# Cross-attentions: half of the next pair's first turning round on either side of a weighting's last block of keys

## The chip, the cores and the metric

The kernel runs on one core of a Trainium2 chip. Its time is the device time of one launch in microseconds (us): 1676.99 us as the median of 3 runs (1670.87 to 1678.79). Engines are called as in the profile: PE (TensorE, matmuls), PEld (TensorE's weight loads), PEldq (its queue of instructions), DVE (VectorE), ACT (ScalarE), POOL (GpSimd), SP (the queue of DMAs).

## The reference

Four decoder layers run one after the other on a batch of 8 sequences of 56 tokens, 256 wide, each layer with a self-attention, an attention or another mixing over the outside context `ctx_512`, and a feed-forward block, each with a residual and a layer norm. Layers 0, 2 and 3 have a cross-attention of the same form (16 heads, latent keys of width 64, 1500 keys):

```
scores = einsum('bhsr,bhlr->bhsl', q_r, k_r)
attn   = softmax(scores, axis=-1)
ctx_c  = einsum('bhsl,bld->bhsd', attn, kv_rope)
out    = einsum('bhsd,hkd->bshk', ctx_c, w_kc_kv).reshape(b, s, H*K) @ Wo.T
```

All three run through the same function of the kernel, `cross_attention`, and this is the only function that the change touches.

## The kernel before, in words

**Pairs.** The 8 sequences go in 4 couples (`j`, two sequences `e` = 0 and 1, one on partitions 0 to 63 and one on 64 to 127 of the operands). 16 heads times 56 tokens are 896 rows of scores for each sequence, cut into 7 pieces of 128 rows. One piece for both sequences of a couple is a pair in the sense of this document: `NU` = 28 pairs `i` in each cross-attention, 84 in the kernel. In every seventh (`u` = 3, `SPLIT`) the 128 rows belong to two halves of the heads, so that the weighting has four parts of 64 columns where it has two of 128 otherwise. Below these are the split pairs.

**Steps of a pair.** (1) `score` (L1019): six matmuls of 64 rows and 500 columns fill PSUM banks 0 to 2 (`e` = 0) and 3 to 5 (`e` = 1). The profile shows each as two records. (2) `rowmax` on DVE (L1299, L1301, L1304): row maxima, for `e` = 0 bank by bank, for `e` = 1 in one. (3) `exp` on ACT (L1220): one for each `e`, with the row sum read out after it. (4) `normalise` on DVE (L1308, L1312). (5) `turn` on PE (L1106): the weights are transposed in blocks of 125 keys, 24 blocks of two transposes each (one from partitions 0 to 63, one from 64 to 127), in three rounds `k` of 8 blocks. Round 0 writes banks 0 and 1, the banks of the scores of `e` = 0. (6) The copies of the turned blocks to SBUF: round 0 by DVE (L1318), rounds 1 and 2 by ACT (L1227). (7) `weigh` on PE (L1119): for 12 blocks of keys, the context (125 rows, 64 columns) is the stationary operand and the turned weights stream past. Two parts of a block write the two halves of the columns of bank 6, and each is again two records. The last one raises `pv_mm`. (8) `keep` on DVE (L1325) copies bank 6 away, and POOL (L892) sets it in place.

**Order on PE.** It is written out by hand: in step `i` of the loop PE issues `score(i)`, then `weigh(i - 2)`, then the three rounds of `turn(i - 1)`. The 26 steps with `i` from 2 to 27 have all three, so there are 78 in the kernel. Round 0 waits (L1092, L1094) for both divisions of its own pair and for the first exp of the pair scored last, since that exp still reads banks 0 to 2. Round 2 waits for `kept` (L1096), since it writes bank 6, and for the second exp of the pair scored last (L1101). On DVE the order in step `i` is: row maxima of `i`, division `e` = 0, `keep(i - 2)`, the two copies of turned blocks of `i - 1`, division `e` = 1. On ACT: both exps of `i`, then four copies of `i - 1`.

```
        for i in range(1, NU):
            for k in range(3):
                score(i, k)
            ...
            if i >= 2:
                weigh(i - 2)
            for k in turn_order(i - 1):
                turn(i - 1, k)
```

After the loop the last pairs, the projections (L1134) and the norms follow, and the change leaves them alone.

Of the kernel before, what the change touches and what calls it, by code (L numbers as in the profile page):

```python
# [25 lines left out]
L, LC, LT = 1500, 64, 12  # L26
# [138 lines left out]
def keep_busy(c, bank, n, rhs=None, cols=512):  # L165


    rhs = c.ctx_feat[:, 0, :] if rhs is None else rhs
    for _ in range(n):
        c.nc.tensor.matmul(c.ps[:, bank, 0:cols], c.ident[:], rhs[:, 0:cols], start=True, stop=True, skip_group_check=True)  # L170
# [578 lines left out]
def cross_attention(c, name, o, rope, now, prefetch):  # L749
# [19 lines left out]
    else:  # L769
# [33 lines left out]
    maxed, turned_lo, turned_hi, d_in, a_in, pv_mm, kept, ct_in, ct_last = (  # L803
        s.sem(x) for x in ("maxed", "turned_lo", "turned_hi", "d_in", "a_in", "pv_mm", "kept", "ct_in", "ct_last"))
# [8 lines left out]
    def turn_bank(i, k, r):  # L813

        if i == 0:
            return ((0, 1), (2, 5), (6, 7))[k][r]
        if i == NU - 1:
            return ((2, 3), (4, 7), (6, 5))[k][r]
        return ((0, 1), (2, 7), (6, 5))[k][r]
# [14 lines left out]
    def turn_order(i):  # L834

        return (2, 0, 1) if i == 0 else (0, 1, 2)
# [15 lines left out]
    def parts(u):  # L852

        if u == SPLIT:
            return [(0, 0, 0, 64), (1, 1, 0, 64), (0, 1, 64, 128), (1, 0, 64, 128)]
        return [(0, 0, 0, 128), (1, 1, 0, 128)] if u < SPLIT else [(1, 0, 0, 128), (0, 1, 0, 128)]
# [39 lines left out]
    def _(pe):  # L896
# [108 lines left out]
        def score(i, k):  # L1005

            if i == 0 and k < 2:
                pe.wait_ge(cm_act.handle, cm_act.at(2 - k))
            if i > 0 and k == 0:
                for e in range(2):  # L1010
                    pe.wait_ge(exped[e].handle, exped[e].at(i))
            if i > 1 and k < 2:
                pe.wait_ge(d_in.handle, d_in.at(2 * (i - 2) + 1 + k))
            if i > 1 and k == 2:
                pe.wait_ge(a_in.handle, a_in.at(4 * (i - 2) + 3))
            j, u = i // UNITS, i % UNITS
            q = q2[:, j, :, :].rearrange("p h t -> p (h t)")[:, u * 128:(u + 1) * 128]
            for e in range(2):
                m = nc.tensor.matmul(sc[e][:, k, :], q[e * 64:(e + 1) * 64],  # L1019
                                     c.ctx_feat[e * 64:(e + 1) * 64, j, k * 4 * LP:(k + 1) * 4 * LP],  # L1020
                                     start=True, stop=True)
                if e == 0:
                    m.then_inc(*scored[0].next())
                elif k == score_order(i)[-1]:
                    m.then_inc(*scored[1].next())
# [59 lines left out]
        out_of_context(2)  # L1085
        out_of_context(3)

        def turn(i, k):

            if k == turn_order(i)[0]:  # L1090
                for e in range(2):
                    pe.wait_ge(normed[e].handle, normed[e].at(i + 1))  # L1092
            if k == 0 and i < NU - 1:
                pe.wait_ge(exped[0].handle, exped[0].at(i + 2))  # L1094
            if k == 2 and i > 0:
                pe.wait_ge(kept.handle, kept.at(i))  # L1096
            if i == 0 and k == 2:
                pe.wait_ge(lat_in.handle, lat_in.at(4 * NH // 2))
                pe.wait_ge(cm_act.handle, cm_act.at(3))
            if k == (1 if i == 0 else 2) and i < NU - 1:  # L1100
                pe.wait_ge(exped[1].handle, exped[1].at(i + 2))  # L1101
            for n in range(8):
                e, l = divmod(8 * k + n, LT)
                for r in range(2):
                    rows = slice(r * 64, (r + 1) * 64)
                    m = nc.tensor.transpose(c.ps[0:LP, turn_bank(i, k, r), n * 64:(n + 1) * 64],  # L1106
                                            probs[i % 2][e][rows, l * LP:(l + 1) * LP], c.ident[rows, rows])
                    if n == 7:
                        m.then_inc(*(turned_hi if r else turned_lo).next())

        def weigh(i):

            j, u = i // UNITS, i % UNITS
            pe.wait_ge(a_in.handle, a_in.at(4 * (i + 1)))
            pe.wait_ge(d_in.handle, d_in.at(2 * (i + 1)))
            y = c.ps[:, 6, :]
            for l in range(LT):
                for r, e, lo, hi in parts(u):
                    m = nc.tensor.matmul(y[r * 64:(r + 1) * 64, lo:hi], c.ctx_pos[:, j, l, e, :],  # L1119
                                         pT[i % 2][:, lo // 64:hi // 64, LT * e + l, :], start=(l == 0 and lo == 0),  # L1120
                                         stop=(l == LT - 1), skip_group_check=True)
            m.then_inc(*pv_mm.next())

        def project(j):

# [13 lines left out]
# [3 lines that stand above are left out]
            if i == 1:  # L1142

                pe.wait_ge(cm_act.handle, cm_act.at(3))
                keep_busy(c, 6, 1)
                keep_busy(c, 6, 1, None, 256)
            if i >= 2:
                weigh(i - 2)
            for k in turn_order(i - 1):
                turn(i - 1, k)  # L1150
        pe.wait_ge(d_in.handle, d_in.at(2 * (NU - 1)))
        project(0)
        weigh(NU - 2)
        project(1)
        for k in range(3):
            turn(NU - 1, k)
        project(2)
        weigh(NU - 1)
        for j in range(3):
            norm_turn(c, s, pe, j)  # L1160
# [1804 lines left out]
```

## Time and profile before

| what | value |
|---|---|
| median of 3 runs | 1676.99 us (1670.87 to 1678.79) |
| the profiled execution, its own time | 1670.51 us |
| its span, first to last instruction | 1668.7 us |
| PE busy | 1624.9 us, 97% of the span |
| DVE busy | 1112.9 us, 67% |
| ACT busy | 748.2 us, 45% |
| POOL busy | 239.3 us, 14% |
| mean granted clock of TensorE | 0.993 of full speed |

The table is an average over stages. Weight loads (PEld) overlap the matmuls. The end of a matmul in the profile is modelled, and successive ones overlap, so a start less the start before it is the time that a matmul takes in a stream, and the duration given for one record is longer than that. The time outside the span is 1670.51 - 1668.7 = 1.8 us.

### The profile page before, as it was taken

Reading aid. Unit: us, or ns where it says so; the run is one execution under the profiler, and the core shown is the slowest. Engines: PE = TensorE matmul, PEld = TensorE weight load, DVE = VectorE, ACT = ScalarE, POOL = GpSimd, SP = SyncE. Lnnn points to the kernel's source line nnn. Section 1 sums busy time; section 2 is a strip of 40 time slices with the busy share of each in tenths; the row PEclk is TensorE's granted clock in tenths of the full one; section 3 lists DMA queues with packets and bytes.
Section 4 is the critical chain, followed back from the end, with each engine's and each line's share of the span. In section 5 each row is a group of like instructions: output and inputs, shape, how many; then the busy total and the mean of one; then the engine's idle time right before and its main releaser. Section 6 shows DMA issues by size and latency. Waiting matters only on the chain.

```text
span 1668.7 us, 35613 instructions
## 1 busy us (share of the span) xinstructions
PE 1624.9 (97%) x15226; PEld 1104.2 (66%) x15226; DVE 1112.9 (67%) x1964; ACT 748.2 (45%) x1288; POOL 239.3 (14%) x428
## 2 busy tenths in 40 slices
PE   8999999999999889999999999999999999999998
PEld 5575367777755656655367777764566767777765
DVE  2735899999566753266899999535445289999632
ACT  2213366666412641134366666312444366666411
POOL 0011200000010313011200000010455000000030
PEclk9999999999999999999999999999999999999999
DMA  9212020000040011051020000050300220000010
GB/s 279 73 26 82 1 77 2 2 2 2 2 187 1 2 59 40 1 118 63 1 96 2 2 2 2 2 241 1 64 1 1 114 89 2 2 2 2 2 45 11
DMA packets 35494, 71.10 MB, mean 43 GB/s; under 512 B 25331, under 2 KB 29747, under 8 KB 31405
## 3 DMA queue, kind: packets, MB, share of 16 engines
q1 hardware_dynamic: 35338, 68.83, 12.7%
q8 instruction: 121, 1.98, 0.5%
q14 instruction: 35, 0.29, 0.1%
HBM read 68.36 MB, written 0.46 MB: 41 GB/s over the span
## 4 chain that ended last, share of the span: by engine, by line
PE 90%; DVE 5%; ACT 2%; issue 1%; DMA 1%; POOL 1%; ACTq 0%; DVEq 0%; SPq 0%; POOLq 0%
PE ps L1106 14%; PE ps L1119 14%; PE ps L1019 13%; PE ps L351 10%; PE ps L1478 9%; PE ps L930 3%; PE ps L2549 3%; PE ps L1134 3%; PE ps L513 2%; PE ps L1918 2%; PE ps L940 1%; PE ps L2576 1%; PE ps L966 1%; PE ps L951 1%; PE ps L508 1%
## 5 line engine op out<-in xcount | busy, mean ns | idle before, releaser
L1220 ACT ACTIVATE arena<-ps,softmax_stats 128x1500 f32<-128x1500 f32 x168 | 254.0, 1512 | 192.8 <-DVE softmax_stats L1301 190.8
L1119 PEld LDWEIGHTS ps<-arena,ctx_pos 125*64 125x64 f32 x4608 | 222.3, 137 | 58.4 <-issue 55.4
L1106 PE MATMUL ps<-ident,arena 64*125 64x64 f32 x4032 | 239.2, 271 | 1.9 <-ACT arena L1220 1.6
L1119 PE MATMUL ps<-arena,ctx_pos 125*64 125x128 f32 (+1 forms) x4608 | 240.5, 262 | 0.0
L1106 PEld LDWEIGHTS ps<-ident,arena 64*125 64x125 f32 x4032 | 226.8, 185 | 17.0 <-issue 13.5
L1019 PE MATMUL ps<-ctx_feat,arena 64*128 64x500 f32 x1008 | 230.5, 590 | 0.0
L1227 ACT COPY arena<-ps 125x512 f32<-125x512 f32 x336 | 172.5, 599 | 77.8 <-PE ps L1106 77.8
L1299 DVE TENSOR_REDUCE softmax_stats<-ps 128x1 f32<-128x500 f32 x252 | 170.7, 678 | 48.9 <-PE ps L1019 48.5
L351 PE MATMUL ps<-arena 128*128 128x256 f32 x736 | 174.6, 383 | 2.9 <-ACT arena L2644 1.0
L1312 DVE TENSOR_SCALAR arena<-arena,softmax_stats 128x1500 f32<-128x1500 f32 x168 | 168.3, 1002 | 5.9
L1478 PE MATMUL ps<-x_feat,arena 128*128 128x448 f32 (+1 forms) x416 | 166.2, 544 | 1.2 <-DVE arena L1579 1.2
L351 PEld LDWEIGHTS ps<-arena 128*128 128x128 f32 x736 | 137.0, 190 | 40.2 <-issue 16.9
L892 POOL COPY arena<-arena 64x128 f32<-64x128 f32 (+1 forms) x186 | 51.3, 276 | 682.1 <-DVE arena L1325 675.9
L1304 DVE TENSOR_REDUCE softmax_stats<-ps 128x1 f32<-128x1500 f32 x84 | 143.6, 1709 | 0.0
L1019 PEld LDWEIGHTS ps<-ctx_feat,arena 64*128 64x128 f32 x1008 | 89.2, 187 | 80.0 <-issue 77.1
L1478 PEld LDWEIGHTS ps<-x_feat,arena 128*128 128x128 f32 (+1 forms) x416 | 78.7, 191 | 64.6 <-issue 60.6
L1318 DVE COPY arena<-ps 125x512 f32<-125x512 f32 x168 | 107.6, 682 | 12.8 <-PE ps L1106 12.5
L1545 ACT ACTIVATE arena<-ps 128x448 f32<-128x448 f32 (+1 forms) x52 | 28.3, 544 | 193.0 <-PE ps L1478 192.9
L1579 DVE TENSOR_TENSOR arena<-ps,arena 128x448 f32<-128x448 f32 x45 | 28.1, 624 | 129.5 <-ACT arena L1545 94.6
L930 PE MATMUL ps<-x_feat,arena 128*128 128x448 f32 x128 | 56.1, 563 | 0.2
L2549 PE MATMUL ps<-x_feat,arena 128*128 128x448 f32 x128 | 52.4, 552 | 1.2 <-issue 0.7
L2677 DVE TENSOR_TENSOR arena<-ps,arena 128x448 f32<-128x448 f32 x32 | 20.0, 625 | 46.0 <-ACT arena L2621 45.9
(319 smaller groups left out, 1923.4 us busy)
## 6 DMA issues: line engine op xcount, KB each, us to landing
ctx_pos<-in_ctx SPq DMA_DIRECT2D x1, 2688.0 KB
arena<-in_L1f_gate SPq DMA_DIRECT2D x1, 2304.0 KB, 12.0
arena<-in_L1f_up SPq DMA_DIRECT2D x1, 2304.0 KB, 17.0
arena<-in_L1f_down SPq DMA_DIRECT2D x1, 2304.0 KB, 7.8
arena<-in_L0a_Wq SPq DMA_DIRECT2D x1, 2048.0 KB, 10.5
arena<-in_L0a_Wc SPq DMA_DIRECT2D x1, 2048.0 KB, 19.4
arena<-in_L0x_Wq SPq DMA_DIRECT2D x1, 2048.0 KB, 10.1
arena<-in_L0x_Wo SPq DMA_DIRECT2D x1, 2048.0 KB, 8.4
```

The source lines that it names most:

```text
L351: m = c.nc.tensor.matmul(y_of(c, s, j), lhsT, rhs, start=False, stop=last, skip_group_check=True)
L930: m = nc.tensor.matmul(c.ps[:, 2 + h % 2, 0:NT], wq[:, k, h, :], c.x_feat[:, k, :, 0:T], start=(k == 0), stop=(k == KT - 1))
L1019: m = nc.tensor.matmul(sc[e][:, k, :], q[e * 64:(e + 1) * 64], c.ctx_feat[e * 64:(e + 1) * 64, j, k * 4 * LP:(k + 1) * 4 * LP], start=True ...
L1106: m = nc.tensor.transpose(c.ps[0:LP, turn_bank(i, k, r), n * 64:(n + 1) * 64], probs[i % 2][e][rows, l * LP:(l + 1) * LP], c.ident[rows, r ...
L1119: m = nc.tensor.matmul(y[r * 64:(r + 1) * 64, lo:hi], c.ctx_pos[:, j, l, e, :], pT[i % 2][:, lo // 64:hi // 64, LT * e + l, :], start=(l = ...
L1220: nc.scalar.activation(probs[i % 2][e].rearrange("p (k l) -> p k l", k=3), sc[e], ACT.Exp, bias=low[:, i % 4, e:e + 1], accum_out=total[:, ...
L1227: nc.scalar.copy(pT[i % 2][:, r, 8 * k:8 * k + 8, :], c.ps[0:LP, turn_bank(i, k, r), :].rearrange("p (s q) -> p s q", s=8)).then_inc(*a_in ...
L1299: nc.vector.tensor_reduce(peak[:, i % 4, k:k + 1], sc[0][:, k, :], AX.X, ALU.max).then_inc(*maxed.next())
L1304: nc.vector.tensor_reduce(low[:, i % 4, 1:2], sc[1], AX.XY, ALU.max, negate=True).then_inc(*lowered[1].next())
L1312: nc.vector.tensor_scalar(probs[i % 2][e], probs[i % 2][e], inv[:, i % 4, e:e + 1], None, ALU.mult).then_inc(*normed[e].next())
L1318: nc.vector.tensor_copy(pT[i % 2][:, r, 0:8, :], c.ps[0:LP, turn_bank(i, 0, r), :].rearrange("p (s q) -> p s q", s=8)).then_inc(*d_in.next())
L1478: m = nc.tensor.matmul(c.ps[0:m_, bank(n) + i, 0:NT], w[:, k, n * 128:n * 128 + m_], c.x_feat[:, k, :, 0:T], start=(k == 0), stop=(k == KT ...
```

## The change

Step `i` of the loop, from `i` = 2 on, calls `weigh_and_turn(i - 2)`. PE then issues: the weighting's blocks of keys 0 to 10; the waits of turning round 0; the first 4 blocks of that round (8 transposes); the weighting's last block of keys, 11; the other 4 blocks of the round; rounds 1 and 2 as before. Step 1 and all that comes after the loop keep their order. The instructions, operands, banks and semaphores are the same ones. The other engines' programs are unchanged.

```
-        def turn(i, k):
+        def turn_ready(i, k):
             ... (the waits of turn, as before)
-            for n in range(8):
+
+        def turn_blocks(i, k, ns):
+
+            for n in ns:
                 e, l = divmod(8 * k + n, LT)
                 ...
+        def weigh_keys(i, ls):
+
+            j, u = i // UNITS, i % UNITS
             y = c.ps[:, 6, :]
-            for l in range(LT):
+            for l in ls:
                 for r, e, lo, hi in parts(u):
                     m = nc.tensor.matmul(...)
-            m.then_inc(*pv_mm.next())
+            if LT - 1 in ls:
+                m.then_inc(*pv_mm.next())
...
+        def weigh_and_turn(i):
+
+            weigh_ready(i)
+            weigh_keys(i, range(LT - 1))
+            turn_ready(i + 1, 0)
+            turn_blocks(i + 1, 0, range(4))
+            weigh_keys(i, [LT - 1])
+            turn_blocks(i + 1, 0, range(4, 8))
+            for k in (1, 2):
+                turn(i + 1, k)
...
             if i >= 2:
-                weigh(i - 2)
-            for k in turn_order(i - 1):
-                turn(i - 1, k)
+                weigh_and_turn(i - 2)
+            else:
+                for k in turn_order(i - 1):
+                    turn(i - 1, k)
```

## Rows read from the trace of the kernel before

**Rows 1.** Busy time of each engine in the loop of the first cross-attention.

```profile
core 0: us, PE busy (x) PEld busy (x) DVE busy (x) ACT busy (x) POOL busy (x), PEclk, DMA share, GB/s
226.60:435.30 208.70, 208.70 (x2990) 163.30 (x2988) 191.76 (x310) 135.27 (x206) 16.52 (x60) 1.00 0.01 3
```

**Rows 2.** The page's chain of work that ended last, by engine.

```profile
PE 90%; DVE 5%; ACT 2%; issue 1%; DMA 1%; POOL 1%; ACTq 0%; DVEq 0%; SPq 0%; POOLq 0%
```

**Rows 3.** Timeline of PE, one pair's period: start us, us, engine, line.

```profile
389.22 2.84 PE L1119 MATMUL ps<-arena,ctx_pos 125*64 125x128 f32 x48
391.99 2.83 PE L1106 MATMUL ps<-ident,arena 64*125 64x64 f32 x48
394.66 2.73 PE L1019 MATMUL ps<-ctx_feat,arena 64*128 64x500 f32 x12
397.33 0.88 PE L1119 MATMUL ps<-arena,ctx_pos 125*64 125x128 f32 x12
```

**Rows 4.** L1119's and L1106's records, 389 to 398 us: ns minimum/median/maximum.

```profile
L1119 PE MATMUL ps<-arena,ctx_pos x60: 272/273/323, 389.2 to 397.9; 125*64 125x128 f32 x60
L1106 PE MATMUL ps<-ident,arena x48: 269/269/317, 392.0 to 394.6; 64*125 64x64 f32 x48
```

**Rows 5.** Timeline of PE, a split pair.

```profile
421.64 3.02 PE L1119 MATMUL ps<-arena,ctx_pos 125*64 125x64 f32 x96
424.58 2.83 PE L1106 MATMUL ps<-ident,arena 64*125 64x64 f32 x48
```

**Rows 6.** Timeline of PE where a projection (L1134) stands between other matmuls.

```profile
434.92 0.60 PE L1106 MATMUL ps<-ident,arena 64*125 64x64 f32 x8
435.45 0.65 PE L1134 MATMUL ps<-arena 128*64 128x256 f32 x4
...
438.31 0.82 PE L1134 MATMUL ps<-arena 128*64 128x256 f32 x6
438.96 0.50 PE L1119 MATMUL ps<-arena,ctx_pos 125*64 125x128 f32 x6
...
457.63 1.47 PE L1134 MATMUL ps<-arena 128*64 128x256 f32 x12
459.03 0.48 PE L186 MATMUL ps<-x_tok,ident 128*128 128x256 f32 x1
```

**Rows 7.** L1134's record durations; PEld's row at the last of these changes.

```profile
L1134 PE MATMUL ps<-arena x32: 379/379/430, 455.4 to 458.7; 128*64 128x256 f32 x32
...
459.03 0.51 PEld L186 LDWEIGHTS ps<-x_tok,ident 128*128 128x128 f32 x3 [0.38 <-issue]
```

**Rows 8.** Timeline of ACT, end of the first exp of a pair, ordinary and split.

```profile
391.64 0.19 ACT L1220 ACTIVATION_READ_ACCUMULATOR arena<-ps,softmax_stats 128x1 f32 x1
...
424.05 0.19 ACT L1220 ACTIVATION_READ_ACCUMULATOR arena<-ps,softmax_stats 128x1 f32 x1
```

**Rows 9.** The wait of L1094 in PE's queue, whole trace.

```profile
L1094 PEldq EVENT_SEMAPHORE  x78: 51/51/51, 229.3 to 1562.0; - x78
```

**Rows 10.** A wait of the same kind on which an idle PE stood, and its release.

```profile
522.78 0.60 ACT L2067 COPY arena<-arena 128x448 f32<-128x448 f32 x1
...
L2115 PEldq EVENT_SEMAPHORE  x1: 51/51/51, 523.4 to 523.4; - x1
...
523.50 0.19 PEld L2118 LDWEIGHTS ps<-arena 128*128 128x128 f32 x1 [1.67 <-ACT arena L2164]
```

**Rows 11.** Timeline of DVE from `keep` to the next pair's first maximum.

```profile
392.98 0.28 DVE L1325 COPY arena<-ps 128x128 f32<-128x128 f32 x1
393.18 1.28 DVE L1318 COPY arena<-ps 125x512 f32<-125x512 f32 x2
394.38 0.15 DVE L1308 RECIPROCAL softmax_stats<-softmax_stats 128x1 f32<-128x1 f32 x1
394.57 1.00 DVE L1312 TENSOR_SCALAR arena<-arena,softmax_stats 128x1500 f32<-128x1500 f32 x1
395.75 0.68 DVE L1299 TENSOR_REDUCE softmax_stats<-ps 128x1 f32<-128x500 f32 x1 [0.19 <-PE ps L1019]
```

More of the change, by code:

```diff
@@ L1109, in turn, with weigh_ready @@
                         m.then_inc(*(turned_hi if r else turned_lo).next())
-        def weigh(i):
-            j, u = i // UNITS, i % UNITS
+        def turn(i, k):
+            turn_ready(i, k)
+            turn_blocks(i, k, range(8))
+        def weigh_ready(i):
             pe.wait_ge(a_in.handle, a_in.at(4 * (i + 1)))
             pe.wait_ge(d_in.handle, d_in.at(2 * (i + 1)))
+        def weigh_keys(i, ls):
+            j, u = i // UNITS, i % UNITS
             y = c.ps[:, 6, :]
-            for l in range(LT):
+            for l in ls:
                 for r, e, lo, hi in parts(u):
@@ L1121, in weigh @@
                                          stop=(l == LT - 1), skip_group_check=True)
-            m.then_inc(*pv_mm.next())
+            if LT - 1 in ls:
+                m.then_inc(*pv_mm.next())
+        def weigh(i):
+            weigh_ready(i)
+            weigh_keys(i, range(LT))
+        def weigh_and_turn(i):
+            weigh_ready(i)
+            weigh_keys(i, range(LT - 1))
[5 more added lines that the diff above has]
+                turn(i + 1, k)
         def project(j):
```

## The prediction

> **What bounds the kernel now.** I read the page's chain first: nine tenths of it is PE's [rows 2]. Then the busy time in the loop of a cross-attention [rows 1]; the loops at 848 and 1356 us give the same to 0.1 us. PE is busy for all of the 208.70 us, DVE for 191.76, ACT for 135.27, and the granted clock is 1.00, the upper level of 2.4 GHz. So in the stage of the change nothing hides time added to PE's stream, and nothing but PE's own work can be cut. Last I read the timeline of one pair [rows 3]. From one weighting's start to the next it is 397.33 - 389.22 = 8.11 us, 7.78 of it DVE's by its instructions. That leaves two questions: what it costs PE to go from one kind of matmul to the other, which the change does twice more for each pair, and whether PE has what it needs when the first turning round is issued one block of keys earlier.
>
> **The change part by part.** No instruction is added or taken away; DVE, ACT, POOL and SP keep their programs, and no DMA is moved. Each of the 78 steps [rows 9] changes PE's order: 11 blocks of keys, wait, 4 turning blocks, 1 block of keys, 20 turning blocks, where it was 12, wait, 24.
>
> *A block of keys, and a turning block.* A start plus the group's time less one record's duration is the last start of the group. The weighting's last record starts at 389.22 + 2.84 - 0.27 = 391.79, the turning's at 391.99 + 2.83 - 0.27 = 394.55 [rows 3, 4]. In both groups records go in pairs side by side, 24 in each group. The turning's 23 steps take 2.56 us; the first is 0.05 longer (below), so one step is 0.109 us. The weighting's step is the same: (2.57 - 0.05) / 23. A turning block is one step. A block of keys is two, 0.22 us (split pair: 48 steps in 3.02 us, 0.058 each, 0.23 for a block [rows 5]).
>
> *The switch between shapes.* From the weighting's last start to the turning's first is 391.99 - 391.79 = 0.20 us [rows 3], where a step is 0.11: 0.09 extra. And the first record of each group is longer than the others, 323 against 273 ns and 317 against 269 [rows 4]; by that 0.05 the second pair is late. A switch costs 0.14 us. Is that a wait in disguise? The wait of L1094 stands in front of the turning, so I looked at other places. In a split pair the exp that it waits for ends 424.58 - (424.05 + 0.19) = 0.34 us ahead of the turning, in an ordinary one 391.99 - (391.64 + 0.19) = 0.16 ahead [rows 5, 8]. Yet the switch is no shorter there: last start 421.64 + 3.02 - 0.22 = 424.44, so 0.14 to 0.15 for a step of 0.058, again 0.09 extra. From transposes to a full-height matmul of 64 columns, the direction that the change adds and the loop doesn't have, the projection shows it: last start 434.92 + 0.60 - 0.27 = 435.25, next 435.45, 0.09 extra, and the first record 0.05 longer [rows 6, 7]. From the projection to the weighting, one shape to the same shape, there is none: 438.31 + 0.82 - 0.38 = 438.75, next 438.96, which is the 0.21 of its 256 columns [rows 6, 7]. From the projection to another shape where the profile names no releaser but "issue" it is back: 457.63 + 1.47 - 0.38 = 458.72, next 459.03, 0.31 for 0.21 [rows 6, 7]. So the price goes with the change of shape and not with a wait. Two more switches for each pair: 78 x 2 x 0.142 = **+22.2 us**. Below: 0, if a load could be had under the stream. Above: no row of such a switch without a wait exceeds this, so the same.
>
> *The wait of the first round, one block of keys earlier.* The exp's row sum ends at 391.83 [rows 8]. How soon after such a release PE can start is seen where it stood idle on a wait of the same kind: ACT's copy ends at 522.78 + 0.60 = 523.38, the load starts at 523.50 [rows 10]: 0.11 to 0.12 us. In the loop the turning can then start no sooner than 391.83 + 0.115 = 391.945. Before, PE reaches it at 391.99, free of stall by 0.045 us. The change reaches it one block of keys sooner, at 391.77, and stands for 0.17 us. Exp follows from the scores of its pair through the maximum, all of which are timed from the scores' end, so a longer period doesn't help: the stall comes again in each pair. In a split pair the margin was 0.34 - 0.115 = 0.22 us and the block is 0.23: a stall of 0.01. The split pairs are 4 of 26 in each loop, 12 of 78. Sum: 66 x 0.17 + 12 x 0.01 = **+11.4 us**. Below 0, if PE took the release at once and the exp ended sooner; above the whole block, 66 x 0.22 + 12 x 0.23 = 17.3. I take 11.4, by the row.
>
> *What is queued behind.* Behind the wait stand the 4 turning blocks, the last block of keys and the rest. `pv_mm` comes later: from the turning's start 0.05 + 4 x 0.109 + 0.09 + 0.16, so 0.74 us after it where it was 0.2 before it. DVE's copy began at 393.18, 0.38 us after the start of the turning's eighth block (391.99 + 0.05 + 7 x 0.109 = 392.80) [rows 3, 11], so a reader follows a matmul's start by 0.38 at most. `keep`, which DVE took 392.98 - 391.99 = 0.99 us after the turning's start, held by its division, may so be at 0.74 + 0.38 = 1.12, up to 0.13 late, well ahead of the copies. Round 0 is complete 0.22 + 0.28 = 0.50 us later from the same start. DVE's copies and its second division are then at most 0.50 later, and the next scores and their first maximum are 0.50 later as well, so DVE goes on waiting for PE by the 0.19 us or more that it has now [rows 11]. Round 2 begins 0.5 us further behind the second exp and `kept`. ACT's copies move with rounds 1 and 2. So nothing else becomes late: cost 0, hidden by the half microsecond that PE itself lost.
>
> *Sum.* An ordinary pair 0.17 + 0.285 = +0.455 us, a split one +0.295: 66 x 0.455 + 12 x 0.295 = 30.0 + 3.5 = **+33.6 us**. The profiled execution took 1670.51 us (span 1668.7 and 1.8 outside) and would take 1704.1. The median is 6.5 above that execution; on it, 1676.99 + 33.6 = **1710.6 us**.
>
> *A rule that would say otherwise.* Rows 3 to 7 show a switch at 0.14 us with and without a wait in front. The Trainium skill, "TensorE: Matmul & The Clock Gate", Step-by-step, says that weight loads are pulled ahead of running matmuls where the row groups don't conflict or the load goes to the background buffer; by that alone the added switches would be free and the sum would be the stall's. The Trainium skill, "TensorEngine Tiling (Array Packing)", Key Properties, has the opposite: "Changing tiling mode (not just tile) drains the TensorE". The rows side with the second, at 0.14 us each.
>
> **The rivals.** *(A) The added switches are hidden*, at least mostly: only the stall is left, +11.4, or 1688.4 us. For it: turning to scores, two shapes of 64 rows, costs only the 0.05 (394.66 - 394.55 = 0.11) [rows 3]. Against it: every row of this very kind of switch.
>
> *(B) Not slower: DVE sets the pace.* If DVE's chain (7.78 of 8.11 us) governed the period, PE would have half a microsecond of hidden slack in its modelled ends, and 0.45 more would vanish in it: 0 us, 1677. It would decide from the point where DVE no longer waits for the scores. Against it: DVE waits for PE ahead of each pair's first maximum, by 0.19 us [rows 11], and a split weighting, longer by 0.17 us (421.64 to 424.58 is 2.94, against 2.77), starts its turning later by just that [rows 3, 5].
>
> *(C) A second wait*: the first round, split in two, is complete so late that DVE ends its second division after the next scores are ready. My margin of 0.19 us would have to be wrong by more than itself; a loss of 0.3 us for each pair on top gives 78 x 0.3 = 23, 1734 us.
>
> **How the numbers follow.** Forecast 0.83, A 0.08, B 0.04, C 0.05. The range for 8 in 10: from half of the added switches hidden (33.6 - 11 = 22.6, rounded with the scatter of the three runs to 1697) to the stall at its upper bound (22.2 + 17.3 = 39.5, 1716.5), so 1697 to 1717. A measurement tells this kernel from no change from about 0.5%, 8.4 us. Slower by more: forecast, A and C, 0.95. Within: most of B, 0.04. Faster: 0.01.
>
> **What would show it.** In the changed trace a period of some 8.56 us for an ordinary pair (8.58 for a split one, from 8.11 + 0.17 = 8.28); 8 transposes, then 4 weighting records, then 40 transposes; ahead of the first 8 an idle step of about 0.37 us from the weighting's last start (0.20 before), with ACT's exp as releaser; 0.20 us at each of the two inner switches and a longer first record behind each; each loop longer by 11.2 us, PE still without other gaps, DVE's wait ahead of the first maximum at 0.2 to 0.3 us. The rest of the kernel is unchanged to a microsecond. Inner steps of 0.11 would prove A. The forecast is wrong if the loops grow by less than 7 or more than 14 us each.

## The result, and the profile after

The changed kernel takes 1712.33 us (median of 4 runs, 1702.21 to 1715.0) against 1677.89 us (4 runs, 1670.87 to 1679.0). The ratio is 1.0215, 95% interval 1.0181 to 1.025: 2.15% slower, which on 1677.89 is 36 us. The forecast was 33.6.

The loops of the three cross-attentions account for it. I take a loop from the first record of its first weighting to the first record of the projection behind it, in the timeline of PE: 226.62 to 435.45 = 208.83 us before [rows 6 has the end], and after:

```profile
223.53 0.33 PE L1130 MATMUL ps<-arena,ctx_pos 125*64 125x128 f32 x2
...
444.54 0.44 PE L1163 MATMUL ps<-arena 128*64 128x256 f32 x2
```

That is 221.01 us. In the same way all three loops make 626.5 us before and 663.0 after: **+36.5 us**. They give the same to 0.02 us each, and a comparison of loops is free of what the rest of the kernel does from run to run. The busy time in the first loop (columns: the stretch, its length, then busy time and count of each engine, granted clock, DMA share, GB/s) answers to [rows 1]:

```profile
223.50:444.50 221.00, 218.12 (x2990) 165.94 (x2988) 195.81 (x310) 135.32 (x206) 16.44 (x60) 1.00 0.01 3
```

The same 2990 records of PE, but 2.9 us of idle time have appeared in a stage that had none. The other 9.3 of the 12.2 us stand as busy: the ends of matmuls are modelled, and they reach into the gaps between the starts. ACT and POOL do what they did. DVE's 195.81 us for 191.76 are the same 310 records too: their durations add up to 201.6 us for 201.1, but less of them overlaps. The timeline of PE for one pair (start us, us) answers to [rows 3]:

```profile
395.51 2.62 PE L1130 MATMUL ps<-arena,ctx_pos 125*64 125x128 f32 x44
398.27 0.65 PE L1109 MATMUL ps<-ident,arena 64*125 64x64 f32 x8
398.85 0.44 PE L1130 MATMUL ps<-arena,ctx_pos 125*64 125x128 f32 x4
399.21 2.40 PE L1109 MATMUL ps<-ident,arena 64*125 64x64 f32 x40
401.45 2.73 PE L1019 MATMUL ps<-ctx_feat,arena 64*128 64x500 f32 x12
404.11 1.09 PE L1130 MATMUL ps<-arena,ctx_pos 125*64 125x128 f32 x16
```

The period is 404.11 - 395.51 = 8.60 us where it was 8.11 and 8.56 was forecast. Last starts are read as before: the weighting's first part at 395.51 + 2.62 - 0.27 = 397.86, so 0.41 us to the first transpose (0.20 before); the 8 transposes' at 398.27 + 0.65 - 0.27 = 398.65, 0.20 to the last block of keys; that block's at 399.02, 0.19 to 0.20 to the other 40. A longer first record stands at each switch:

```profile
L1109 PE MATMUL ps<-ident,arena x48: 269/269/318, 398.3 to 401.3; 64*125 64x64 f32 x48
...
L1130 PE MATMUL ps<-arena,ctx_pos x48: 272/273/323, 395.5 to 399.0; 125*64 125x128 f32 x48
```

The wait in front of the first transposes, in the timeline of all engines, answers to [rows 8, 10]:

```profile
397.75 0.39 PE L1130 MATMUL ps<-arena,ctx_pos 125*64 125x128 f32 x4
397.93 0.19 ACT L1250 ACTIVATION_READ_ACCUMULATOR arena<-ps,softmax_stats 128x1 f32 x1
...
398.24 0.43 PEld L1109 LDWEIGHTS ps<-ident,arena 64*125 64x125 f32 x6 [0.34 <-issue]
398.27 0.43 PE L1109 MATMUL ps<-ident,arena 64*125 64x64 f32 x4
```

The exp's row sum ends at 397.93 + 0.19 = 398.12, the load starts 0.11 to 0.12 us later, and the first transpose another 0.03 later. The profile puts this idle time down to "issue"; the release has to be seen in ACT's row.

DVE, which answers to [rows 11], goes on waiting for PE:

```profile
399.33 0.29 DVE L1355 COPY arena<-ps 128x128 f32<-128x128 f32 x1
399.90 1.29 DVE L1348 COPY arena<-ps 125x512 f32<-125x512 f32 x2 [0.27 <-PE ps L1109]
...
401.29 1.00 DVE L1342 TENSOR_SCALAR arena<-arena,softmax_stats 128x1500 f32<-128x1500 f32 x1
402.54 0.68 DVE L1329 TENSOR_REDUCE softmax_stats<-ps 128x1 f32<-128x500 f32 x1 [0.25 <-PE ps L1019]
```

The profiled execution of after took 1715.0 us with a span of 1713.2, 44.5 over the span before; 8.0 of that lies outside the loops. The stretches ahead of the first and the second loop are 3.1 and 1.5 us shorter, and the one from the second loop's end to the third's start takes 312.1 us where it took 299.5, 12.6 more, in a stage that the change doesn't touch. Its granted clock is lower (after, then the same work before):

```profile
1322.00:1344.00 22.00, 20.39 (x151) 16.79 (x150) 6.81 (x19) 4.29 (x9) 0.15 (x1) 0.81 0.55 216
1344.00:1388.00 44.00, 42.47 (x221) 26.16 (x220) 16.99 (x26) 21.62 (x49) 0.00 (x0) 0.86 0.20 76
```

```profile
1302.00:1324.00 22.00, 20.87 (x185) 17.28 (x183) 5.96 (x12) 6.67 (x16) 0.15 (x1) 1.00 0.55 216
1324.00:1356.00 32.00, 30.47 (x183) 17.00 (x182) 16.67 (x25) 18.98 (x42) 0.00 (x0) 1.00 0.23 87
```

It belongs to that execution: a kernel below whose loops take the same time as the changed kernel's (663.2 us) ran its profiled execution in 1702.23 us, at a mean granted clock of 0.997 instead of 0.990, and passed that stretch in 298.5 us at a clock of 1.00. The changed kernel's own four runs go the same way: 1702.21 us at 0.997, 1711.06 at 0.993, 1713.6 and 1715.0 at 0.990.

### The profile page after: what moved, and what is told of

Same layout as the page of the kernel before. It is cut to its first block, busy times and chain, and to the rows that moved or that the text cites. A ratio compares the mean times of both kernels' runs of the same rounds, so it can differ in the third digit from the quotient of the medians.

```text
span 1713.2 us, 35613 instructions
## 1 busy us (share of the span) xinstructions
PE 1656.7 (97%) x15226; PEld 1116.9 (65%) x15226; DVE 1124.6 (66%) x1964; ACT 747.5 (44%) x1288; POOL 238.8 (14%) x428
## 4 chain that ended last, share of the span: by engine, by line
PE 89%; DVE 5%; ACT 2%; issue 2%; POOL 1%; DMA 1%; DVEq 0%; ACTq 0%; SPq 0%; POOLq 0%
PE ps L1109 14%; PE ps L1130 14%; PE ps L1019 13%; PE ps L351 9%; PE ps L1508 9%; PE ps L930 3%; PE ps L2579 3%; PE ps L1163 3%; PE ps L513 2%; PE ps L1948 2%; PE ps L940 1%; POOL arena L1782 1%; PE ps L2606 1%; PE ps L1001 1%; PE ps L966 1%
## 5 line engine op out<-in xcount | busy, mean ns | idle before, releaser
L1109 PE MATMUL ps<-ident,arena 64*125 64x64 f32 x4032 | 256.3, 273 | 10.5 <-ACT arena L1250 1.6
L1109 PEld LDWEIGHTS ps<-ident,arena 64*125 64x125 f32 x4032 | 235.5, 186 | 40.6 <-issue 36.1
L1130 PE MATMUL ps<-arena,ctx_pos 125*64 125x128 f32 (+1 forms) x4608 | 257.7, 263 | 0.0
```

## The experiments

The theory: in each pair a stall on the exp's release, and two switches of shape at 0.14 us each. The rival: no stall, all is the price of cutting the two groups. Each kernel is the changed one with the edit shown, unless the text says otherwise. The results are given together after the expectations. The column "loops" is the sum over the three loops of the profiled execution, read as above, "ratio" that of all runs to runs of the kernel before on the same chip.

**The stall filled, with the same switches.**

```
             weigh_ready(i)
+            weigh_keys(i, [0])
             weigh_keys(i, range(LT - 1))
```

> As the changed kernel, but block of keys 0 is weighted twice at the start of each of the 78 weightings (the second overwrites the first), so that PE reaches the wait of turning round 0 one block (0.22 us) later, as in the kernel before. Theory (a stall on the exp's release plus two shape switches at 0.14 us): the added block fills the stall, so each ordinary pair is 0.22 + 0.285 = 0.50 us over before, 78 x 0.50 = 39 us in all, only 3 us over the changed kernel's 36.5 in the loops; the idle step ahead of the first 8 transposes falls from 0.40 to 0.20 us. Rival (no stall; the changed kernel's 0.49 us per pair is all price of the two switches): the block comes on top, 78 x 0.22 = 17 us over the changed kernel, 54 us over before.

**The wait alone, with no added switch.**

```
             turn_ready(i + 1, 0)
-            turn_blocks(i + 1, 0, range(4))
             weigh_keys(i, [LT - 1])
-            turn_blocks(i + 1, 0, range(4, 8))
+            turn_blocks(i + 1, 0, range(8))
```

> The wait of turning round 0 stands ahead of the weighting's last block of keys, as in the changed kernel, but nothing is interleaved: 11 blocks of keys, wait, 1 block, 24 turning blocks. Theory: a stall in each pair and no added switch. With the release to start time of the changed trace (0.145 us) the last block waits 0.30 us in an ordinary pair (no switch hides in the stall here) and 0.13 in a split one: 66 x 0.30 + 12 x 0.13 = 21 us over before. Rival (the switches are everything, the wait is hidden): same time as before.

**A block more, in the order of before.**

```
             weigh_ready(i)
-            weigh_keys(i, range(LT - 1))
+            weigh_keys(i, [0])
+            weigh_keys(i, range(LT))
             turn_ready(i + 1, 0)
-            turn_blocks(i + 1, 0, range(4))
-            weigh_keys(i, [LT - 1])
-            turn_blocks(i + 1, 0, range(4, 8))
+            turn_blocks(i + 1, 0, range(8))
```

> Order of the kernel before, but with block of keys 0 weighted twice in each of the 78 weightings. It measures the price of one block with no wait and no switch added: 66 x 0.219 + 12 x 0.234 = 17.2 us over before by every theory, if PE sets the pace. If DVE set the pace, nothing.

**The switches alone.** `spare_block` weighs keys 0 once more, into columns of bank 6 that nobody reads; its definition is left out here. With `False`, block 11 doesn't raise `pv_mm`; the spare block does, so `keep` comes as late as in the changed kernel.

```
-            weigh_keys(i, range(LT - 1))
+            weigh_keys(i, range(LT), False)
             turn_ready(i + 1, 0)
             turn_blocks(i + 1, 0, range(4))
-            weigh_keys(i, [LT - 1])
+            spare_block(i)
             turn_blocks(i + 1, 0, range(4, 8))
```

> All 12 blocks of keys, the wait, 4 turning blocks, a spare thirteenth block (keys 0 again, into unused columns of bank 6, its result is not used), 20 turning blocks. It has the two added switches and an added block but reaches the wait as late as the kernel before. Theory: 17.2 us for the block and 78 x 0.285 = 22.2 us for the switches, 39.4 us over before, 22 over the kernel with the block more and no interleaving. Rival (all of the changed kernel's loss is switches, 0.49 us per pair): 17.2 + 38 = 55 us over before. Rival (switches are free, all is stall): 17 us.

**The stall made longer by a block.**

```
-            weigh_keys(i, range(LT - 1))
+            weigh_keys(i, range(LT - 2))
...
-            weigh_keys(i, [LT - 1])
+            weigh_keys(i, [LT - 2, LT - 1])
```

> As the changed kernel, but two blocks of keys stand behind the wait: 10 blocks, wait, 4 turning blocks, blocks 10 and 11, 20 turning blocks. Same number of switches. Theory: the stall grows by a whole block in each pair, 0.20 + 0.22 = 0.42 us in an ordinary one and 0.04 + 0.23 in a split one, so the loops take 17 us more than the changed kernel's, 54 us over before; the last start of the weighting to the first transpose becomes 0.62 us, the time from the exp's row sum to the first transpose stays 0.145. Rival (the loss comes from cutting the weighting and the round in two, whatever the cut): no change from the changed kernel, 36 to 37 us over before.

**Four switches in place of two.** The edit is to the kernel with two blocks behind the wait, the one just above.

```
             turn_ready(i + 1, 0)
-            turn_blocks(i + 1, 0, range(4))
-            weigh_keys(i, [LT - 2, LT - 1])
+            turn_blocks(i + 1, 0, range(2))
+            weigh_keys(i, [LT - 2])
+            turn_blocks(i + 1, 0, range(2, 4))
+            weigh_keys(i, [LT - 1])
             turn_blocks(i + 1, 0, range(4, 8))
```

> As the kernel with two blocks of keys behind the wait, but these two are apart: 10 blocks, wait, 2 turning blocks, block 10, 2 turning blocks, block 11, 20 turning blocks. Four added switches where that one has two, the same stall. Theory: 78 x 0.292 = 23 us over that kernel, 77 over before. Rival (a switch costs only where a semaphore wait stands in front of it, the rest being its first record alone, 0.05): 78 x 0.1 = 8 us over that kernel.

**The exp asked for first.**

```
+            if k == 0 and i < NU - 1:
+                pe.wait_ge(exped[0].handle, exped[0].at(i + 2))
             if k == turn_order(i)[0]:
                 for e in range(2):
                     pe.wait_ge(normed[e].handle, normed[e].at(i + 1))
-            if k == 0 and i < NU - 1:
-                pe.wait_ge(exped[0].handle, exped[0].at(i + 2))
```

> As the changed kernel, but turning round 0 asks for the exp ahead of the two divisions. The wait for the exp may then sit on the first weight load itself and not in the separate instruction ahead of it. Elsewhere in the trace of before a load that carries the exp's wait itself starts 0.05 us after the row sum's end, where the separate instruction makes it 0.11 and the matmul 0.145. Theory: 0.145 becomes 0.05 to 0.08, so 0.07 to 0.09 us less in each of 66 ordinary pairs, 5 to 6 us less than the changed kernel in the loops. Rival (the waits are placed alike whatever the order in the program, or the hand-over isn't what counts): no change.

**The block behind the whole round.**

```
-            turn_blocks(i + 1, 0, range(4))
+            turn_blocks(i + 1, 0, range(8))
             weigh_keys(i, [LT - 1])
-            turn_blocks(i + 1, 0, range(4, 8))
```

> As the changed kernel, but the last block of keys stands behind the whole of turning round 0, not in its middle. Same wait, same stall, same number of switches. Theory: the loops take what the changed kernel's take, 36 to 37 us over before; `keep` comes 0.4 us later and DVE's wait ahead of the next first maximum shrinks to some 0.1 us, still not the pace. Rival (the half round on either side matters, or DVE becomes late): another 5 us or more, one way or the other.

**The exp asked for first, in the kernel before.** The same edit, in `turn` of the kernel before.

> The kernel before with the one edit that took 6.4 us from the changed kernel's loops: turning round 0 asks for the exp ahead of the two divisions, and the release to start time falls to 0.05 us. Theory: before the change PE came to that wait after its release, and the 0.20 us from the weighting's last start to the first transpose are all step and switch, so nothing changes: loops 626.5 us, gap 0.20 us. Rival (the 0.20 us hold a wait of up to 0.09): the gap falls towards 0.11 us and the loops by up to 66 x 0.09 = 6 us; then this kernel would be the fastest of all.

| kernel | loops, us | over before | expected by the theory | ratio, 95% interval |
|---|---|---|---|---|
| before | 626.5 | | | |
| changed | 663.0 | 36.5 | 33.6 (forecast) | 1.0215 (1.0181 to 1.025) |
| stall filled | 666.5 | 40.0 | 39 | 1.0252 (1.0208 to 1.0297) |
| wait alone | 651.9 | 25.4 | 21 | 1.0127 (1.0075 to 1.0179) |
| a block more | 643.7 | 17.2 | 17.2 | 1.0099 (1.0062 to 1.0136) |
| switches alone | 666.5 | 40.0 | 39.4 | 1.0226 (1.0179 to 1.0274) |
| two blocks behind | 680.3 | 53.8 | 54 | 1.0323 (1.0267 to 1.0378) |
| two blocks apart | 703.1 | 76.6 | 77 | 1.0435 (1.0397 to 1.0474) |
| exp first | 656.6 | 30.1 | 5 to 6 under changed, 30.5 to 31.5 | 1.0162 (1.0131 to 1.0193) |
| behind the round | 663.2 | 36.7 | 36 to 37 | 1.018 (1.015 to 1.0209) |
| before, exp first | 626.5 | 0.0 | 0 | 0.9995 (0.9955 to 1.0035) |

**What follows.** *The price of a switch.* "Switches alone" less "a block more" is 22.8 us for 156 switches: 0.146 us each. "Two blocks apart" less "two blocks behind" is another 156 switches with other neighbours, and 22.8 us again. Timeline of PE in the kernel with the switches alone:

```profile
394.88 2.84 PE L1130 MATMUL ps<-arena,ctx_pos 125*64 125x128 f32 x48
397.65 0.65 PE L1109 MATMUL ps<-ident,arena 64*125 64x64 f32 x8
398.23 0.44 PE L1141 MATMUL ps<-arena,ctx_pos 125*64 125x128 f32 x4
398.60 2.39 PE L1109 MATMUL ps<-ident,arena 64*125 64x64 f32 x40
```

From the last start of the weighting, 394.88 + 2.84 - 0.27 = 397.45, it is 0.20 us to the first transpose, as before the change, though all that follows is as in the changed kernel. With four switches each of them shows 0.20, with no semaphore wait in front of the inner ones, so the rival for that kernel (a switch without a wait costs its first record alone, 8 us in all) is out:

```profile
399.59 0.43 PE L1109 MATMUL ps<-ident,arena 64*125 64x64 f32 x4 [0.35 <-ACT arena L1252]
399.95 0.44 PE L1130 MATMUL ps<-arena,ctx_pos 125*64 125x128 f32 x4
400.32 0.43 PE L1109 MATMUL ps<-ident,arena 64*125 64x64 f32 x4
400.68 0.44 PE L1130 MATMUL ps<-arena,ctx_pos 125*64 125x128 f32 x4
```

*The price of the stall.* 36.5 - 22.8 = 13.7 us are left for it. A block of keys in front of the wait costs 17.2 us where PE isn't standing ("a block more"), and 3.5 where it is ("stall filled" over changed): 13.7 us of it go into the stall. Two blocks behind the wait add 17.3 us, a whole block for each pair. The first two agree to 0.1 us, and so do the third and the price of a block. The rival would have had 54, 55 and 36 to 37 us over before for "stall filled", "switches alone" and "two blocks behind". The two blocks' stall, in PE's timeline:

```profile
392.94 2.40 PE L1130 MATMUL ps<-arena,ctx_pos 125*64 125x128 f32 x40
395.69 0.65 PE L1109 MATMUL ps<-ident,arena 64*125 64x64 f32 x8 [0.35 <-ACT arena L1250]
396.27 0.66 PE L1130 MATMUL ps<-arena,ctx_pos 125*64 125x128 f32 x8
```

From the last start, 392.94 + 2.40 - 0.27 = 395.07, it is 0.62 us. The first transpose stays where the exp puts it, 2.75 us after the weighting's start (395.69 - 392.94), as in the changed kernel (398.27 - 395.51 = 2.76). Only now, with a stall of 0.4 us, does the profile name ACT.

*The wait alone* cost 25.4 us, 4.4 more than expected. The stall itself is as computed. Timeline of PE:

```profile
391.96 3.19 PE L1130 MATMUL ps<-arena,ctx_pos 125*64 125x128 f32 x48
395.08 2.83 PE L1109 MATMUL ps<-ident,arena 64*125 64x64 f32 x48
```

The last weighting record starts at 391.96 + 3.19 - 0.27 = 394.88, and the last block, which begins two starts earlier by the exp's release (2.75 us after 391.96, at 394.71), takes 395.08 - 394.71 = 0.37 us up to the first transpose, where one step and a switch are 0.11 + 0.20 = 0.31. That is 0.06 us for each pair, 78 x 0.06 = 4.7 us: starting again behind a stall costs more than the stall. Most of it is a longer first record, as behind a switch: the first records of the last block are 295 and 323 ns long where the others are 273, so the block's second starts come at 394.84 and 394.88, the later of them 0.05 us late, though the shape didn't change. In the changed kernel the matmul behind the stall is also the first of a new shape, so this 0.05 us is in the switch already.

*The hand-over.* In the changed kernel the wait for the exp stands in an instruction of its own ahead of the first load. The case of [rows 10] is of this kind, and its first matmul, in the timeline of all engines of before, starts 523.53 - 523.38 = 0.15 us after the release, as in the changed kernel:

```profile
523.53 0.61 PE L2118 MATMUL ps<-arena 128*128 128x448 f32 x1 [1.46 <-ACT arena L2067]
```

With the exp asked for first, the wait for it sits on the first load. All engines, the kernel with the exp first:

```profile
403.90 0.19 ACT L1250 ACTIVATION_READ_ACCUMULATOR arena<-ps,softmax_stats 128x1 f32 x1
...
404.14 0.29 PEld L1109 LDWEIGHTS ps<-ident,arena 64*125 64x125 f32 x4 [0.28 <-ACT arena L1250]
404.14 0.32 PE L1109 MATMUL ps<-ident,arena 64*125 64x64 f32 x2
```

From the row sum's end, 404.09, to the first transpose is 0.05 us in place of 0.145, and the loops take 6.4 us less, a little more than the 5 to 6 expected. In the kernel before the same edit changes nothing in the loops (timeline of PE):

```profile
389.15 2.84 PE L1119 MATMUL ps<-arena,ctx_pos 125*64 125x128 f32 x48
391.92 2.83 PE L1106 MATMUL ps<-ident,arena 64*125 64x64 f32 x48
```

The last start is 391.72, the gap 0.20 us as before. So PE came to that wait after its release, and the 0.20 us before the change were all step and switch. Its ratio, 0.9995, can't be told from 1; no version beats the kernel before.

*Half a round on either side* is no part of the price: with the whole round ahead of the block the loops take 663.2 us. `keep` came later and DVE's wait ahead of the first maximum fell from 0.25 to 0.18 us (0.1 was expected), still a wait for PE:

```profile
399.70 0.29 DVE L1354 COPY arena<-ps 128x128 f32<-128x128 f32 x1 [0.41 <-PE ps L1130]
...
402.47 0.68 DVE L1328 TENSOR_REDUCE softmax_stats<-ps 128x1 f32<-128x500 f32 x1 [0.18 <-PE ps L1019]
```

## Why the prediction was right

- **Bound: PE's stream, with nothing to hide behind.** Right. A block more in each weighting costs its full 17.2 us, which a pace set by DVE (rival B) would have hidden.
- **A block of keys and its step, 0.22 and 0.109 us.** Right, by the same 17.2 us.
- **Two switches at 0.142 us, 22.2 us.** Measured 0.146 and 22.8. The Trainium skill's pull-ahead of weight loads ("TensorE: Matmul & The Clock Gate", Step-by-step), on which rival A rested, gives nothing at a change of shape here; the measured 0.146 us with no wait in front agrees with the drain at a change of tiling mode in "TensorEngine Tiling (Array Packing)", Key Properties.
- **The stall, 11.4 us.** Right in kind, 2.3 too small: 13.7. The term that was mis-sized is the time from the release to the start, 0.115 us, which was read as far as the weight load's start. Behind a stall the first matmul starts another 0.03 us after the load: 398.24 and 398.27. The first matmul of [rows 10]'s case is not in those rows, but the trace of before has it (under "the hand-over"), and with it the right term. With 0.145 the ordinary pair stalls 0.20 us (forecast 0.17), the split one 0.04 (forecast 0.01): 66 x 0.20 + 12 x 0.04 = 13.7.
- **Nothing else late.** Right. DVE waits 0.25 us for the scores where 0.19 or more was forecast; `keep` came 399.33 - 398.27 = 1.06 us after the turning's start, with 1.12 as the forecast's limit. Rival C is out.
- **The sum.** 36.5 us in the loops for 33.6, and 36 us by the ratio. The time of 1710.6 us stands on the median of the first runs; 1712.33 was measured. That these two are only 1.7 us apart is in part luck, since the changed kernel's own runs span 12.8 us; the loops, 2.9 us off, are the test of the sum. The profiled execution gained 44.5, of which 8.0 lie outside the loops: the signs named in the forecast hold for the loops (12.2 us each for 11.2), but "the rest is unchanged to a microsecond" did not, since one execution's granted clock isn't the next one's. The idle step ahead of the first transposes was also to have ACT's exp as its releaser; the profile says "issue" there, and names ACT only in the kernels with two blocks behind the wait or the exp first.

## What to carry to other kernels

Before issuing a consumer earlier in an in-order stream, take the time from its release to its present start: here 0.16 us, of which 0.145 were needed, so the turning could move 0.015 us ahead at most and a block of 0.22 was moved across. In a stream of PE without gaps such a move had nothing to win either: asking for the exp first in the kernel before altered its loops by 0.0 us. Each alternation between matmuls of different shape (64 rows by 125 columns and 125 rows by 64 columns here) cost 0.146 us, the same in two pairs of kernels (from turning to scores, both of 64 rows, the step stayed at 0.11 us), so small pieces of one kind are not to be put between pieces of the other. Where a wait does bind, put the semaphore that comes last on the instruction itself: asked for first, the exp was handed over 0.095 us sooner here.

## What the runs showed of the hardware

- A wait in an instruction of its own hands over in 0.145 us from the release to the first matmul, a wait carried by the weight load in 0.05 us. Here the exp's wait took the first place when it was asked for last of three, and the second when it was asked for first.
- After a stall on the first kind, the two matmuls that run side by side on the halves of the array run 0.03 to 0.04 us out of step until the next change of shape. The later one's first record is longer by 0.05 us also without a change of shape; in "the wait alone" the block behind the stall took 0.06 us more.
- In the changed kernel a stall of 0.20 us on a wait in an instruction of its own stands as "issue" in the profile, with no releaser; at 0.42 us ACT was named, and so it was at a wait carried by the load, with the load's engine idle for 0.28 us.
